# The output projection and first norm in four chunks of tokens, with the first layer's loads and the bias moved into the causal attention

## The reference, cut to what matters

```python
x = L0_attn_x                                   # (2, 1024, 128)
x = _layernorm(x + _L0_attn_ref(x, w_qkv, b_qkv, w_out, b_out))
x = _layernorm(x + _L0_ffn_ref(x, Wqkv, q_scale, k_scale, Wo, ln_g, ln_b, W1, b1, W2, b2))
...
# _L0_attn_ref ends in:
out = jnp.einsum('bsi,oi->bso', o, w_out) + b_out
# _layernorm: (x - mean) / sqrt(var + 1e-5), over the 128 features
```

## Time and profile before

| | us |
|---|---|
| median of 3 runs | 2456.55 |
| lowest, highest | 2451.24, 2464.27 |
| the profiled execution | 2461.72 |
| its span in the trace | 2459.9 |

### The profile page before, as it was taken

The page is one execution under the profiler, slowest core; times in us unless marked ns, Lnnn a source line. Parts: engine busy times, 40 slices in busy tenths (PEclk is TensorE's granted clock), DMA queues, the critical chain, the costliest instruction groups (busy, mean ns, idle before and its releaser), DMA issues. The chain is left out here.

```text
span 2459.9 us, 55624 instructions
## 1 busy us (share of the span) xinstructions
PE 2049.9 (83%) x20371; PEld 1369.4 (56%) x20371; DVE 1858.0 (76%) x3667; ACT 1636.6 (67%) x3009; POOL 1226.2 (50%) x1091
## 2 busy tenths in 40 slices
PE   4389889638999999999999999999999999843390
PEld 2133333214677776777766767766767766632260
DVE  4555663249999999999999999999999999524523
ACT  2035655427888888888888888888888888712020
POOL 0100000047766777776777776677776677300115
PEclk8569997769999999999999999999999999966595
DMA  2403110031110112110211011111211011003102
GB/s 80 89 5 40 26 17 3 3 128 34 36 36 28 36 36 76 32 36 28 81 36 36 28 60 51 33 36 36 72 36 36 28 36 36 27 17 92 50 29 55
DMA packets 70913, 103.25 MB, mean 42 GB/s; under 512 B 21686, under 2 KB 45884, under 8 KB 70108
## 3 DMA queue, kind: packets, MB, share of 16 engines
q1 hardware_dynamic: 68980, 96.29, 14.4%
q0 software_dynamic: 1664, 3.41, 0.6%
HBM read 41.66 MB, written 8.06 MB: 20 GB/s over the span
## 5 line engine op out<-in xcount | busy, mean ns | idle before, releaser
L755 PE MATMUL pA<-layer_weights,x_feature_major 128*128 128x512 f32 x768 | 399.9, 603 | 32.3 <-DMA window_mask<-in_mask_dram 16.2
L1328 POOL TENSOR_TENSOR qk<-rot_cos,rot_sin 128x512 f32<-128x512 f32 x256 | 323.4, 1274 | 155.7 <-DVE rot_sin L1129 155.7
L399 ACT ACTIVATE probs_by_key<-pT 128x512 f32<-128x512 f32 (+3 forms) x384 | 177.6, 490 | 225.8 <-PE pT L352 192.3
L1127 DVE TENSOR_TENSOR rot_cos<-pA,layer_tab 128x512 f32<-128x512 f32 x384 | 262.9, 685 | 77.6 <-ACT sq L968 71.4
L1338 POOL TENSOR_TENSOR qk<-qk,rnorm 128x512 f32<-128x512 f32 x256 | 263.4, 1045 | 88.7 <-DVE rnorm L1162 88.7
L417 DVE TENSOR_REDUCE minus_max<-pS 128x1 f32<-128x1024 f32 (+7 forms) x256 | 184.6, 754 | 128.0 <-PE pS L326 127.8
L968 ACT ACTIVATE sq<-pA 128x512 f32<-128x512 f32 x384 | 228.7, 596 | 67.7 <-PE pA L755 58.1
L1139 DVE TENSOR_REDUCE sumsq<-sq 128x8 f32<-128x512 f32 x384 | 253.6, 671 | 15.3 <-ACT sq L968 15.2
L1129 DVE TENSOR_TENSOR rot_sin<-pA,layer_tab 128x512 f32<-128x512 f32 x384 | 260.9, 680 | 0.0
L1028 ACT ACTIVATE probsT<-pD 64x512 f32<-64x512 f32 x384 | 226.6, 590 | 44.5 <-PE pD L796 41.0
L1345 POOL TENSOR_TENSOR probs<-probs,row_inverse 128x1024 f32<-128x1024 f32 x96 | 182.6, 1903 | 101.7 <-DVE row_inverse L1198 101.7
(11 more groups left out here) (281 smaller groups left out, 4447.4 us busy)
## 6 DMA issues: line engine op xcount, KB each, us to landing
v_shifted<-v SPq DMA_DIRECT2D x96, 384.0 KB, 3.5
v_shifted<-v SPq DMA_DIRECT2D x95, 128.0 KB, 3.4
layer_weights<-in_Wqkv_dram SPq DMA_DIRECT2D x24, 384.0 KB
q_stack<-stacked SPq DMA_DIRECT2D x72, 64.0 KB
k_stack<-stacked SPq DMA_DIRECT2D x72, 64.0 KB
stacked<-part SPq DMA_DIRECT2D x24, 128.0 KB, 1.9
layer_weights<-in_Wo_dram SPq DMA_DIRECT2D x6, 512.0 KB
w_gate<-in_wg_dram SPq DMA_DIRECT2D x8, 256.0 KB, 6.4
```

The source lines that it names most:

```text
L755: pe.matmul(A[c % 2][:, :], cols(X0f, s), slot(s, QKV_AT + 512 * c, 512), start=True, stop=True).then_inc(q_ready[c], 1)
L1127: dve.tensor_tensor(t1[c % 2][:, :].rearrange("p (h g d) -> p h g d", g=2, d=32), a, tabl[s % 2][:, j].unsqueeze(1).broadcast_to([P, 8, 2, ...
L1328: pool.tensor_tensor(qk(s, c), t1[c % 2][:, :], t2[c % 2][:, :], ALU.add).then_inc(added[c], 1)
```

## The change

`project_out`, the first call of `layernorm_all` and `set_aside` become one stage, `project_out_normalized`. It works in four chunks of four token tiles: PE turns and multiplies a chunk, DVE adds the residual, sums and scales to minus the mean, ACT squares each tile with minus the mean as its bias and an accumulated sum, DVE makes the variance, POOL the power, and DVE normalizes tile by tile; the order over the chunks is written out on every engine. SP stores each chunk when it is normalized; nobody in this stage waits for the stores, POOL does so in `window_layers`.

The output weights and bias are loaded in `load_tokens`. The bias is added to `X` by POOL at the start of the causal attention, four instructions of four tiles. The weights of layer 0 and the two tables have SBUF tensors of their own from the start and are loaded by SP in the causal attention, behind the stack loads of the first four groups and ahead of the first `load_maxima`. `load_layer` is otherwise unchanged (it became a function of its own).

```diff
         exp_done = sem("exp_done")
         pv_done = sem("pv_done")
+        biased = sem("residual_biased")
         o_kept = sem("o_kept")
         den_done = sem("den_done")
         block = ctx.enter_context(nc.Block())
@@ -304,6 +305,9 @@
             sp.dma_start(cm[:, :, :], w["causal"]).then_inc(mask_in, 16)
             for g in range(SLOTS_G):
                 load_stacks(g)
+            load_layer(sp, w, env["W0"], 0, env["w0_loaded"])
+            sp.dma_start(env["xpos"][:], w["xpos"]).then_inc(env["const_loaded"], 16)
+            sp.dma_start(env["mask"][:], w["mask"]).then_inc(env["const_loaded"], 16)
             for g in range(GROUPS):
                 load_maxima(g)
                 if g >= 1 and g - 1 + SLOTS_G < GROUPS:
@@ -475,6 +479,10 @@
             for r in range(2):
                 pool.memset(Vs[r][:, :, :, AD:AD + 1], 1.0).then_inc(v_cleared, 1)
             pool.wait_ge(v_cleared, 4)
+            pool.wait_ge(env["out_loaded"], 32)
+            for n in range(4):
+                X4 = env["X"][:, 4 * n:4 * n + 4, :]
+                pool.tensor_tensor(X4, X4, env["bo"][:, :].unsqueeze(1).broadcast_to([P, 4, D]), ALU.add).then_inc(biased, 1)
             for g in range(GROUPS):
                 ge(pool, pv_done, NQ * (g - 1))
                 r0, c0 = (g // 4) * TB, (g % 4) * (GH * AD)
...
+def project_out_normalized(nc, env, w, O):
+    X, ident, wo = env["X"], env["ident"], env["wo"]
+    CH = 4
+    CT = TILES // CH
     ctx = ExitStack()
     with ctx:
         def sb(name, shape, dt=F32):
...
         def sem(name):
             return ctx.enter_context(nc.semaphore(name))
         woT = sb("wo_turned", [P, D])
         OT = sb("o_turned", [P, TILES, P])
+        Z, squares = (sb(n, [P, TILES, D]) for n in ("summed_a", "squares_a"))
+        negm, sq, ve, rstd, half = (sb(n, [P, TILES]) for n in (
+            "negative_mean_a", "square_sum_a", "var_eps_a", "rstd_a", "root_power_a"))
         bank = [ctx.enter_context(nc.psum_tensor(f"pR{r}", [P, 512], F32)) for r in range(8)]
+        w_ready, w_kept, t_ready, t_kept, y_ready = (sem(n) for n in ("w_ready", "w_kept", "t_ready", "t_kept", "y_ready"))
+        added, reduced, centred, squared, eps_done, half_set, rooted, normed = (sem(n) for n in (
+            "added", "reduced", "centred", "squared", "eps_done", "half_set", "rooted", "normed"))
         block = ctx.enter_context(nc.Block())
+        def chunk(n):
+            return slice(n * CT, (n + 1) * CT)
         @block.sync
         def _(sp):
+            for n in range(CH):
+                sp.wait_ge(normed, CT * (n + 1))
+                sp.dma_start(w["aside"][:, chunk(n), :], X[:, chunk(n), :]).then_inc(env["aside_stored"], 16)
         @block.tensor
         def _(pe):
+            def turn(n):
+                for j in range(CT):
+                    mm = pe.transpose(bank[n][:, j * P:(j + 1) * P], O[:, CT * n + j, :], ident[:, :])
+                mm.then_inc(t_ready, 1)
+            def project(n):
+                pe.wait_ge(t_kept, n + 1)
+                for j in range(CT):
+                    mm = pe.matmul(bank[4 + n][:, j * P:(j + 1) * P], OT[:, CT * n + j, :], woT[:, :], start=True, stop=True)
+                mm.then_inc(y_ready, 1)
+            pe.wait_ge(env["out_loaded"], 32)
             pe.transpose(bank[4][:, 0:P], wo[:, :], ident[:, :]).then_inc(w_ready, 1)
+            turn(0)
+            turn(1)
             pe.wait_ge(w_kept, 1)
+            project(0)
+            turn(2)
+            project(1)
+            turn(3)
+            project(2)
+            project(3)
         @block.scalar
         def _(act):
+            def keep(n):
+                act.wait_ge(t_ready, n + 1)
+                act.activation(OT[:, chunk(n), :], bank[n][:, :].rearrange("p (t n) -> p t n", t=CT), AF.Copy).then_inc(t_kept, 1)
+            def square(n):
+                act.wait_ge(centred, n + 1)
+                for t in range(CT * n, CT * n + CT):
+                    act.activation(squares[:, t, :], Z[:, t, :], AF.Square, bias=negm[:, t:t + 1], accum_out=sq[:, t:t + 1])\
+                        .then_inc(squared, 1)
             act.wait_ge(w_ready, 1)
             act.activation(woT[:, :], bank[4][:, 0:P], AF.Copy).then_inc(w_kept, 1)
+            keep(0)
+            keep(1)
+            keep(2)
+            square(0)
+            keep(3)
+            for n in range(1, CH):
+                square(n)
+        @block.gpsimd
+        def _(pool):
+            pool.memset(half[:, :], -0.5).then_inc(half_set, 1)
+            pool.wait_ge(half_set, 1)
+            for n in range(CH):
+                pool.wait_ge(eps_done, n + 1)
+                pool.tensor_tensor(rstd[:, chunk(n)], ve[:, chunk(n)], half[:, chunk(n)], ALU.pow).then_inc(rooted, 1)
         @block.vector
         def _(dve):
+            def residual(n):
                 dve.wait_ge(y_ready, n + 1)
+                dve.tensor_tensor(Z[:, chunk(n), :], X[:, chunk(n), :], bank[4 + n][:, :].rearrange("p (t n) -> p t n", t=CT), ALU.add)\
+                    .then_inc(added, 1)
+                dve.wait_ge(added, n + 1)
+                dve.tensor_reduce(negm[:, chunk(n)], Z[:, chunk(n), :], AX.X, ALU.add).then_inc(reduced, 1)
+                dve.wait_ge(reduced, n + 1)
+                dve.tensor_scalar(negm[:, chunk(n)], negm[:, chunk(n)], -1.0 / D, None, ALU.mult).then_inc(centred, 1)
+            def variance(n):
+                dve.wait_ge(squared, CT * (n + 1))
+                dve.tensor_scalar(ve[:, chunk(n)], sq[:, chunk(n)], 1.0 / D, EPS, ALU.mult, ALU.add).then_inc(eps_done, 1)
+            def normalize(n):
+                dve.wait_ge(rooted, n + 1)
+                for t in range(CT * n, CT * n + CT):
+                    dve.tensor_scalar(X[:, t, :], Z[:, t, :], negm[:, t:t + 1], rstd[:, t:t + 1], ALU.add, ALU.mult).then_inc(normed, 1)
+            residual(0)
+            residual(1)
+            variance(0)
+            residual(2)
+            variance(1)
+            normalize(0)
+            residual(3)
+            variance(2)
+            normalize(1)
+            variance(3)
+            normalize(2)
+            normalize(3)
 def causal_masks():
...
+def load_layer(sp, w, W, l, done):
...
-        W = sb("layer_weights", [P, 2 * SLOT])
+        W = [env["W0"], sb("layer_weights1", [P, LAYER_COLUMNS])]
...
         @block.sync
         def _(sp):
-            load_layer(sp, 0)
-            sp.dma_start(tab[:], w["xpos"]).then_inc(const_loaded, 16)
-            sp.dma_start(mask[:], w["mask"]).then_inc(const_loaded, 16)
-            load_layer(sp, 1)
+            load_layer(sp, w, W[1], 1, w_loaded[1])
             sp.wait_ge(zeroed, 1)
             for s in range(STEPS):
                 if s % TILES == 8 and s > TILES:
                     sp.wait_ge(x2_done, s // TILES * PB)
-                    load_layer(sp, s // TILES + 1) if s // TILES + 1 < DEPTH else None
+                    load_layer(sp, w, W[(s // TILES + 1) % 2], s // TILES + 1, w_loaded[(s // TILES + 1) % 2]) if s // TILES + 1 < DEPTH else None
                 r = s % 3
...
             pool.wait_ge(const_loaded, 32)
             pool.wait_ge(x_turned, 4)
+            pool.wait_ge(env["aside_stored"], 64)
             pool.wait_ge(zeroed, 7)
             pool_body(pool, -1)
...
             sp.dma_start(ident[:, :], w["identity"]).then_inc(loaded, 16)
             sp.dma_start(X[:, :, :], w["x"].rearrange("(t p) d -> p t d", p=P)).then_inc(loaded, 16)
+            sp.dma_start(env["wo"][:, :], w["a_w_out"]).then_inc(env["out_loaded"], 16)
+            sp.dma_start(env["bo"][:, :], w["a_b_out"].rearrange("(a n) -> a n", a=1).broadcast_to([P, D])).then_inc(env["out_loaded"], 16)
             sp.wait_ge(loaded, 32)
...
-def set_aside(nc, w, X):
-    ctx = ExitStack()
-    with ctx:
-        copied = ctx.enter_context(nc.semaphore("copied"))
-        block = ctx.enter_context(nc.Block())
-        @block.sync
-        def _(sp):
-            sp.dma_start(w["aside"], X[:, :, :]).then_inc(copied, 16)
-            sp.wait_ge(copied, 16)
...
-        load_tokens(nc, w, X, ident, identb)
+        for name, shape, dt in (("wo", [P, D], F32), ("bo", [P, D], F32), ("W0", [P, LAYER_COLUMNS], F32),
+                                ("xpos", [P, TB, 4 * DH], F32), ("mask", [P, TB, 4 * WINDOW], BF16)):
+            env[name] = ctx.enter_context(nc.sbuf_tensor(f"{name}_ahead", shape, dt))
+        for name in ("out_loaded", "w0_loaded", "const_loaded", "aside_stored"):
+            env[name] = ctx.enter_context(nc.semaphore(f"{name}_ahead"))
+        load_tokens(nc, env, w, X, ident, identb)
         with ExitStack() as scope:
-            V, O, Z = (tokens(scope, n) for n in ("values", "attended", "summed_a"))
+            V, O = (tokens(scope, n) for n in ("values", "attended"))
             project_heads(nc, env, w, V)
             causal_attention(nc, env, w, V, O)
-            project_out(nc, env, w, O, Z)
```

(3 more changed lines are left out.)

111 lines of the change are left out of this document (39 added, 72 removed).

## The result

The changed kernel takes 2447.21 us, the median of 20 runs (2430.24 to 2469.34), against 2458.23 us for the kernel before in 20 runs beside it (2447.20 to 2485.87). The ratio is 0.9938, with a 95% interval of 0.9915 to 0.9960: 15 us less (2458.23 × 0.0062 = 15.2; the interval is 10 to 21). Ratios here are taken over the executions in the chip's faster state, so they can lie up to 0.002 off the quotient of the two medians. The forecast was 25.2 us less, 2431, with a range of 2419 to 2446; on the median that it started from the ratio gives 2441 (2456.55 × 0.9938). The profiled execution took 2444.69 us (span 2442.9), where the one before took 2461.72 (span 2459.9): 17.0 us less.

What follows compares the result with a forecast made beforehand. Three stretches after attention, 51.9 us with no engine full, were taken as one chain of single steps holding nearly the whole change. A gain of 26.2 us less 1 in the attention, from median 2456.55, gave 2431 us, range 2419 to 2446.

Steps and rivals of the forecast that it cites:

- rival A: The forecast itself: first Q some 26 us earlier, attention late by 3 us at most; 2431, range 2424 to 2438; chance 0.70.
- rival B: Maxima round trip held behind layer's loads: 7.4 us and up, 2438, or 2445 if SP's issue is held; chance 0.17.
- PE's start, the chunked chain, the block's end: After attention: PE starts 3.4 us earlier, DVE's list takes 12.8 us, the block ends at 486.2 against 496.46.
- Rival C: Chunked projection and norm gain nothing, only copy and load wait go: gain 15.9 us, time 2441; chance 0.06.
- a price of splitting: In the norm, 16 normalizing instructions cost DVE 5.0 us where one cost 2.29, outweighed by other engines working beside it.
- ScalarE's square: In the chunked norm, square with accumulated sum: taken as 0.28 us, upper bound 0.56, which would cost 1.5 to 2 us.
- Bias by POOL, copy to HBM, `load_layer(1)`: Bias in the attention, four unwaited stores, and layer 1's loads behind the first Q: each forecast to cost zero.
- The loads of layer 0: Moved from the window layers' entry into the attention: first Q follows the block's start by 8.2 us, not 19.9.
- I take **1 us: Delay of the attention's first maxima read-back by the moved loads, chosen between bounds of 0 and 7.4 us.
- the slack of 6.2: First maxima round trip in the attention: some 6.2 us to spare before PE's matmul at 140.20 needs it.
- The share of 0.53: DMA share during stack loads, 92.0 to 124.6; read as nearer full-rate transfer, though it also agrees with 8 rings.
- one stretch of 6.3 us: Noise in the attention: one half-clock stretch of 20 us more or fewer costs or saves 6.3 us.

Runs made afterwards that it cites:

- Experiment 7: Changed kernel with the 25 loads behind the first maxima round trip and the bias added by DVE in the new stage instead of POOL; 2440.07 us, ratio 0.9912.
- experiment 4: Against the kernel before: only the loads of layer 0 and tables moved ahead of the first maxima, old projection, norm and copy kept; 2451.72 us, ratio 0.9986.
- experiments 3: Changed kernel with the loads of layer 0 and the tables back at the entry of the window layers; 2433.33 us, ratio 0.9919.
- experiments 9 and 10: Changed kernel with only the 15 small loads (9), or only the large ones and tables (10), ahead of the first maxima, the rest behind; 2435.08 and 2448.83 us.
- the loads behind: Changed kernel with the 25 loads issued behind the first maxima round trip, timed three times; ratios 0.9852, 0.9892, 0.9899.
- experiment 8: The kernel before, unaltered, profiled once more; 2468.33 us in a single execution.
- experiments 1 and 11: The changed kernel unaltered, run again in two groups; 2435.44 us, ratio 0.9908, and 2455.07 us, ratio 0.9957.
- groups one and three: Experiments 1 to 4 and 9 to 12, each group on one chip and timed against the kernel before in it: 2455.55 and 2465.88 us.
- experiments 2 and 5: Changed kernel with the 25 loads behind the first maxima round trip, run in two groups; 2417.52 us, ratio 0.9852, and 2433.38 us, ratio 0.9892.

## Why the prediction was partly wrong

The time on the forecast's own median, 2441, lies inside the range of 2419 to 2446, but outside rival A's own 2424 to 2438. It is in the range because the upper end had been set by rival B's price (put at 2439 there, where the working gives 2438), and B is what happened. The stage was forecast rightly, step by step; the loads' new place was not.

**PE's start, the chunked chain, the block's end: right.** Forecast from the end of `attended`: first residual at +4.2 us, next block at +17.5, first Q at +25.7. Measured: +4.4, +17.4, +25.6. DVE's list took 12.2 us, where 12.8 were summed; the four normalizing instructions of a chunk 1.11 us, where 1.25 were taken. The gain from `attended` to the first Q is 26.2 us, as forecast. Rival C (the chain gains nothing) is out.

One reason given for it was wrong. The 16 normalizing instructions were set against one of 2.29 us, as a price of splitting. But each subtracts the mean and scales, so they stand for two instructions of the old norm, and the old sum of squares was a third that ScalarE's accumulated sum takes over. The timeline of the norm before:

```profile
484.37 2.29 DVE L61 TENSOR_TENSOR tokens<-summed_a,norm_a_mean 128x2048 f32<-128x2048 f32 x1
...
488.64 2.29 DVE L63 TENSOR_REDUCE norm_a_var<-values 128x16 f32<-128x2048 f32 x1 [1.97 <-ACT values L73]
```

The 16 took 4.56 us (1.11, 1.10 and 2.35), the two that they replace 4.58, and 2.29 us of DVE went away. So DVE paid no price in this pair of profiles, whatever a small instruction costs by itself.

**ScalarE's square: between its bounds.** It shows 0.39 us from start to start, with a second instruction of 0.19 us that reads the accumulator; I took 0.28 with 0.56 as the upper bound. It makes DVE wait for 0.21, 0.34 and 0.63 us, 1.2 us in all, and still DVE's list came out 0.6 us shorter than summed.

**Bias by POOL, copy to HBM, `load_layer(1)`: zero, right.** POOL's four instructions stand at 77.47 in the changed kernel and take 4.92 us. The first Q doesn't wait for SP. Experiment 7 adds that the bias would have cost nothing on DVE either, since DVE waits for PE at that point.

**The loads of layer 0: right on one side, wrong on the other.** Their wait went: 11.2 us in experiment 4, 11.1 (37.1 - 26.0) between experiments 3 and the whole, where 11.7 were forecast. But "I take **1 us**" for their new place is the step that failed. Measured are 6.6, 9.2 and 10.3 us in three profiles of the changed kernel. The mechanism was rival B, at the chance 0.17, in its dearer form in which SP's own issue is held as well. In the first profile it adds up so: the store went out at 139.87 and not at 130.85 (9.0 us late); it took 4.76 us to land and not 1.44 (3.3); the read-back took 2.1 us and not about 1.7 (0.4). That is 12.7 us, less the slack of 6.2: 6.5, measured 6.57. The sum must come out, since PE reached the matmul at 140.2 both times; what it shows is the share of each part. SP's late issue has the largest, and by itself it exceeds the slack by 2.8 us.

Where was the error in the working? I reckoned with DMA time only: stack loads "that end at 124.6", then 12 us at full rate. That left out SP itself. Right behind the stack loads SP needed 25.5 us to issue 25 loads, and not 14.3 to 14.7, so the store behind them could not even be issued. That SP waits for room in a full queue would explain it, and experiments 9 and 10 fit that; it was not seen directly. The timing of the old place was taken as an upper bound (19.9 us from a queue that was empty), and it wasn't one. The share of 0.53 was a sign of room: the moved loads ran beside the stack loads, at a share of 0.62 to 0.67 up to 124.6 in three profiles of the changed kernel. But room on the DMA engines neither let SP issue faster nor let the store land sooner. The rows were there to warn: in the kernel before SP issued its last stack load at 111.50, but the DMA engines were at work on them long after the earlier trace rows.

**The sum.** 26.2 - 6.6 to 10.3 gives 16 to 20 us for the changed kernel, and its three ratios give 15 (10 to 21), 23 (14 to 31) and 11 (4 to 17) us. For the loads behind, without a wait, 26 us are expected, and the three ratios give 36, 27 and 25 us. Each interval holds what its profile gives, that of the 36 us (26 to 47) only at its edge; they are wide enough to hold a good deal else.

**The clock as noise: the size was too small.** I allowed one stretch of 6.3 us. The granted clock between 140 and 460 was as follows, all in the columns of the earlier trace rows; this work is the same in all kernels, and only its first 10 us differ. The kernel before (experiment 8):

```profile
140.00:460.00 320.00, 288.47 (x1982) 114.11 (x1984) 165.52 (x268) 181.84 (x397) 2.40 (x6) 0.88 0.12 17
```

The changed kernel, experiments 1 and 11:

```profile
140.00:460.00 320.00, 274.32 (x2017) 109.13 (x2018) 166.29 (x271) 184.25 (x403) 2.52 (x7) 0.94 0.13 21
```

```profile
140.00:460.00 320.00, 276.73 (x1973) 110.03 (x1973) 166.59 (x270) 179.39 (x393) 2.40 (x6) 0.91 0.14 23
```

From the first transposed scores to `attended` these took 328.3, 308.0 and 319.2 us. One kernel alone thus spans 308.0 to 320.8 us (experiment 1 and the first profile), twice what I allowed. In each kernel timed six times or more, its time falls by 14 to 25 us for each 0.01 of its mean granted clock (correlation -0.72 to -0.99). Read off at one clock, 0.915, on each kernel's own line, the changed kernel stands 12.5 and 10.3 us under the kernel before in groups one and three, and the loads behind 17.7, 17.5 and 19.6 us; to this belong some 5 and 7 us, since idle stretches at the 0.5 clock that are taken away raise the mean by themselves (26 us of 2450 at 0.5 and not at 0.915 make 0.004). That gives about 17 and 15 us, and about 25, 25 and 27: the sums above, and between the two kernels 7 to 11 us, the size of the wait. This is a fit, not a measurement of the clock's cause.

What stays open: both profiles of the kernel before show 0.88 there, and the twelve of all other kernels 0.89 to 0.95. The loads alone (0.91), the stage alone (0.95) and the bias on DVE (0.91) all lie above, so none of these parts is the cause by itself; it may be chance, or something that all edits share. Open too is why the wait is 2.3 us in experiment 4 and 6.6 to 10.3 in the changed kernel. The last stack load was issued at 111.34 there and at 113.93 to 117.63 here, and SP needed 22.7 us for the 25 loads and not 25.5 to 26.6. The scatter of the last stack load is not of the edits: one and the same kernel, with the loads behind, has it at 118.96, 110.32 and 116.92. The stretch from 92 to 112 in the first two (experiments 2 and 5):

```profile
92.00:112.00 20.00, 11.71 (x43) 4.58 (x44) 11.38 (x16) 0.00 (x0) 0.00 (x0) 0.50 0.53 72
92.00:112.00 20.00, 12.62 (x49) 4.92 (x47) 13.39 (x19) 0.00 (x0) 0.00 (x0) 0.50 0.54 102
```

The DMA engines were as busy, but moved 72 GB/s in one and 102 in the other; over the 14 profiles this rate is 67 to 102 and the lower it is, the later the last stack load (0.2 us apart in the one pair out of order). Why the same transfers are slower in some executions wasn't settled. POOL's bias isn't needed for it: experiment 7, without it there, has 86 GB/s and 114.31. PE's own arrival follows too: it reached its first transposed scores between 139.1 and 140.2 where the last stack load was issued by 115.9, and between 141.5 and 142.8 where it was later, so late stacks cost up to 2.6 us that the column of waits doesn't show.

## What to carry to other kernels

A load moved under other work isn't free because DMA time is free: what counts is the first small, urgent transfer behind it, on SP's order and in the DMA engines' backlog. Before moving bulk loads, look for the next round trip on that queue, compare the time at which its predecessors are issued with the time at which they have landed, and put the bulk loads right behind the round trip. And read the effect where it acts (milestone to milestone), because one pair of executions here differed by 8 us in the attention, which goes with the clock, and by 11 us in a stall that the kernel before has as well.

## What the runs showed of the hardware that I had not expected

- SP's issue slows down behind a backlog: the same 25 loads took it 14.7 us behind a drained queue (the kernel before), 16.1 us behind one round trip, and 22.7 to 26.6 us right behind the stack loads; 15 small ones alone took 17.5 us there.
- A small store behind bulk loads took 4.8 us (changed kernel), 7.7 us (large ones just ahead) and 7.9 us (on ScalarE's queue) until its read-back could go, and 2.80 and 3.45 us behind stack loads that had not yet drained (experiments 2 and 3), against 1.44 us where they had.
- ScalarE's activation with an accumulated sum costs 0.39 us for 128 columns, start to start, against 0.28 for a plain copy; the trace shows the read of the accumulator as an instruction of 0.19 us.
- A stall of 10 to 12 us on ScalarE, ended by something that the profile calls remote, came in every profile of two groups of runs and in none of the other, in the kernel before too.
- The same stack loads kept the DMA engines at the same share (0.53 to 0.54) but moved 67 to 102 GB/s, by the execution.
- The same attention work of one kernel took 308 to 321 us at granted clocks of 0.94 to 0.89.
